# Causal self attention of layers 0 and 2: the mask before the row maximum added by VectorE instead of by identity products

## What is computed

```python
q, k, v = heads(x)                       # 8 batches, 16 heads, 256 rows, 8 columns; layer 2 rotates q and k
att = einsum('bhqd,bhkd->bhqk', q, k) * scale
att = where(causal, att, -inf)
att = softmax(att, axis=-1)              # the kernel takes the row maximum first and subtracts it
y = einsum('bhqk,bhkd->bhqd', att, v)
x = x + y @ w_out
```

## Time and profile before

| | us |
|---|---|
| median of 3 runs (1857.1 to 1859.6) | 1857.48 |
| the profiled execution, its own time | 1858.08 |
| its span in the profile | 1856.2 |
| TensorE busy in the span | 1498.0 |
| VectorE busy | 857.5 |
| ScalarE busy | 700.1 |
| GpSimd busy | 483.3 |

### The profile page before, as it was taken

How to read it: one execution, slowest core, us unless ns; L and a number is a source line. 1 busy time by engine, 2 the same in 40 slices (tenths; PEclk the granted TensorE clock), 3 DMA queues, 4 the chain that set the end, 5 groups by cost and what they waited for, 6 DMA issues and landing times. The chain is left out here.

```text
span 1856.2 us, 29632 instructions
## 1 busy us (share of the span) xinstructions
PE 1498.0 (81%) x10887; PEld 830.3 (45%) x10887; DVE 857.5 (46%) x2404; ACT 700.1 (38%) x1418; POOL 483.3 (26%) x566
## 2 busy tenths in 40 slices
PE   6899899995689999985998899973092579999876
PEld 4344344432544444454456344452071335555545
DVE  4555345542335555555312565355034645554244
ACT  2244414433137767562341143442031314343324
POOL 5533053310021111010001544100652435341034
PEclk9999999997999999986999999985595779999788
DMA  7800000000000000000002200000222000000012
GB/s 212 113 2 1 1 1 1 1 2 1 0 1 1 1 1 1 0 1 1 1 1 95 74 2 1 1 1 2 72 70 63 12 12 7 13 7 1 1 56 79
DMA packets 60258, 42.40 MB, mean 23 GB/s; under 512 B 13188, under 2 KB 54120, under 8 KB 60120
## 3 DMA queue, kind: packets, MB, share of 16 engines
q1 hardware_dynamic: 54752, 32.42, 7.1%
q0 software_dynamic: 3552, 7.33, 1.1%
q10 hardware_dynamic: 1816, 0.81, 0.2%
HBM read 25.88 MB, written 14.66 MB: 22 GB/s over the span
## 5 line engine op out<-in xcount | busy, mean ns | idle before, releaser
L1351 ACT ACTIVATE scores_L_experts_L<-L3x_psL 128x512 f32<-128x512 f32 x128 | 76.5, 597 | 173.2 <-PE L3x_psL L1214 169.5
L1388 DVE CUSTOM_DVE_ANT_0 L3x_junk<-L3x_psS,L3x_mask_rows 128x256 f32<-128x256 f32 x224 | 86.1, 421 | 92.4 <-PE L3x_psS L1176 84.0
L1214 PE MATMUL L3x_psL<-identb,L3x_mask_parts 128*128 128x256 bf16 x768 | 96.2, 276 | 0.0
L894 ACT ACTIVATE L0x_probs<-L0x_psL 128x512 f32<-128x512 f32 x96 | 52.1, 594 | 114.1 <-PE L0x_psL L707 78.9
L894 ACT ACTIVATE L2a_probs<-L2a_psL 128x512 f32<-128x512 f32 x96 | 52.1, 594 | 105.7 <-PE L2a_psL L705 70.9
L894 ACT ACTIVATE L0a_probs<-L0a_psL 128x512 f32<-128x512 f32 x96 | 52.1, 594 | 100.8 <-PE L0a_psL L705 65.0
L1196 PE MATMUL L3x_psL<-L3x_qm,ctx_T 32*128 32x512 f32 x256 | 73.3, 647 | 11.8 <-DVE L3x_mx L1388 11.3
L1214 PEld LDWEIGHTS L3x_psL<-identb,L3x_mask_parts 128*128 128x128 bf16 x768 | 70.4, 98 | 21.5 <-issue 13.7
L1625 PE MATMUL L1a_psL<-L1a_soft_near,neg_tri 128*128 128x512 f32 x128 | 67.9, 612 | 0.2 <-DVE L1a_soft_near L1832 0.2
L2907 POOL DMA_INDIRECT packed_rows<-h,slot x32 | 30.9, 964 | 141.7 <-POOLq L92 132.2
L1176 PE MATMUL L3x_psS<-L3x_km,L3x_qT 32*128 32x512 f32 x224 | 66.2, 668 | 1.9 <-DVE L3x_mx L1388 1.9
(11 more groups left out here) (800 smaller groups left out, 3917.6 us busy)
## 6 DMA issues: line engine op xcount, KB each, us to landing
L2f_rows<-packed_rows SPq DMA_DIRECT2D x8, 325.0 KB, 3.2
packed_rows<-zeros SPq DMA_DIRECT2D x1, 2560.0 KB, 28.2
experts_L_L<-in_L_ffn_w_dram SPq DMA_DIRECT2D x1, 2048.0 KB, 8.5
unpacked_rows<-zeros SPq DMA_DIRECT2D x1, 2048.0 KB, 18.0
scores_L_experts_L<-in_L_ffn_w_dram SPq DMA_DIRECT2D x1, 2048.0 KB, 7.9
L2f_back_rows<-unpacked_rows SPq DMA_DIRECT2D x16, 128.0 KB, 2.6
L3x_mask_rows<-in_mask_Bx1xSxS_ff_dram SPq DMA_DIRECT2D x8, 256.0 KB, 2.9
sorted_rows<-zeros SPq DMA_DIRECT2D x1, 1472.0 KB, 17.9
```

Of the source, the lines that this page charges most:

```text
L894: nc.scalar.activation(probs[:, half, a, k, :], psL[i % RING][:], ACT.Exp, scale=scale).then_inc(s_prob, 1)
L1214: last = nc.tensor.matmul(at[:, :, t * P:(t + 1) * P], parts[:, b % 2, i, t, u * P:(u + 1) * P], two, start=False, stop=i == PARTS - 1, sk ...
L1351: nc.scalar.activation(probs[:, half, a, k, :], psL[i % RING][:], ACT.Exp).then_inc(s_prob, 1)
L1388: last = nc.vector.tensor_tensor_reduce(out=junk[:, i, :], in0=psS[a][:, i * S:(i + 1) * S], in1=mrow[:, b % 2, t, :], scale=1.0, scalar=L ...
```

## The change

`quad_heads` gets an argument `hide_on_dve`, set for L0a and L2a and not for L0x. Where it is set, `hide_score` and the second half of `first_scores` issue nothing, and the products of q and k signal VectorE themselves. VectorE adds the mask to the bank while reading it and writes the sum to one buffer in SBUF, `hidden_scores` (128 x 512, float32); it waits for the add, and reduces the buffer. Before the next add it waits until that reduction is done, since there is one buffer. A new semaphore, `s_free`, counts the banks that have been read (by the add where there is one, by the reduction elsewhere), and TensorE waits for it in place of `s_red`.

```diff
 def quad_heads(nc, mem, w, name, *, ...
-               cross=False, mask, scale, loads=(), clear=()):
+               cross=False, mask, scale, hide_on_dve=False, loads=(), clear=()):
...
-        s_rq, s_rk = sem("q_roped"), sem("k_roped")
+        s_rq, s_rk, s_free = sem("q_roped"), sem("k_roped"), sem("score_bank_read")
+        hidden_scores = sb("hidden_scores", [P, 512]) if hide_on_dve else None
+        on_pe = [s is not None and not hide_on_dve for s in mask.scores]
+        on_dve = [s is not None and hide_on_dve for s in mask.scores]
...
                 def free_score_banks(m):
                     if m >= 1:
-                        pe.wait_ge(s_red, 2 * m)
+                        pe.wait_ge(s_free, 2 * m)
...
                 def hide_score(m, a):
-                    hidden = mask.scores[SCORE_AT[m % SLOTS][1]]
-                    if hidden is not None:
+                    k = SCORE_AT[m % SLOTS][1]
+                    hidden = mask.scores[k]
+                    if on_pe[k]:
                         nc.tensor.matmul(psS[a][:], mem.identb[:], hidden.unsqueeze(1).to_broadcast([P, 4, P]), start=False, stop=True,
                                          skip_group_check=True).then_inc(s_score, 1)
...
+                masked = [0]
+
+                def largest(dst, bank, k, m):
+                    heads = bank[:].rearrange("p (j n) -> p j n", j=4)
+                    if on_dve[k]:
+                        if masked[0]:
+                            dve.wait_ge(s_red, masked[0])
+                        masked[0] += 1
+                        at = hidden_scores[:].rearrange("p (j n) -> p j n", j=4)
+                        nc.vector.tensor_tensor(at, heads, mask.scores[k].unsqueeze(1).to_broadcast([P, 4, P]), ALU.add).then_inc(s_free, 1)
+                        dve.wait_ge(s_free, m + 1)
+                        nc.vector.tensor_reduce(dst, at, AX.X, ALU.max).then_inc(s_red, 1)
+                    else:
+                        nc.vector.tensor_reduce(dst, heads, AX.X, ALU.max).then_inc(s_free, 1)
...
-                        nc.vector.tensor_reduce(dst, psS[a][:].rearrange("p (j n) -> p j n", j=4), AX.X, ALU.max).then_inc(s_red, 1)
+                        largest(dst, psS[a], k, 2 * m + a)
...
                 def gather_max(b):
-                    dve.wait_ge(s_red, ITEMS * (b + 1))
+                    dve.wait_ge(s_free, ITEMS * (b + 1))
+                    if hide_on_dve:
+                        dve.wait_ge(s_red, 2 * sum(on_dve[k] for _, k in SCORE_AT) * (b + 1))
```

More of the change, by code:

```diff
@@ L645, in score @@
                     last = nc.tensor.matmul(psS[a][:], qT[rows, b % 3, t * P:(t + 1) * P], km[rows, b % 3, :, u * P:(u + 1) * P],
-                                            start=True, stop=mask.scores[k] is None, skip_group_check=True)
-                    if mask.scores[k] is None:
+                                            start=True, stop=not on_pe[k], skip_group_check=True)
+                    if not on_pe[k]:
                         last.then_inc(s_score, 1)
                 def hide_score(m, a):
-                    hidden = mask.scores[SCORE_AT[m % SLOTS][1]]
-                    if hidden is not None:
+                    k = SCORE_AT[m % SLOTS][1]
+                    hidden = mask.scores[k]
+                    if on_pe[k]:
                         nc.tensor.matmul(psS[a][:], mem.identb[:], hidden.unsqueeze(1).to_broadcast([P, 4, P]), start=False, stop=True,
@@ L659, in first_scores @@
                     else:
-                        pe.wait_ge(s_red, 4 * k)
+                        pe.wait_ge(s_free, 4 * k)
                     t, u = KINDS[k]
@@ L665, in first_scores @@
                         last = nc.tensor.matmul(first_banks[r][:], qT[rows, 0, t * P:(t + 1) * P], km[rows, 0, :, u * P:(u + 1) * P],
-                                                start=True, stop=hidden is None, skip_group_check=True)
-                        if hidden is None:
+                                                start=True, stop=not on_pe[k], skip_group_check=True)
+                        if not on_pe[k]:
                             last.then_inc(s_score, 1)
-                    if hidden is not None:
+                    if on_pe[k]:
                         for r in range(4):
@@ L3411, in decoder @@
         quad_heads(nc, mem, w, "L0a", wq=W0[:, 0:P], wk=W0[:, P:2 * P], wv=W0[:, 2 * P:3 * P], wo=w["L0_attn_w_proj"][:],
-                   bq=0, bk=1, bv=2, bo=0, mask=causal, scale=qk, loads=first_experts(w, dram),
+                   bq=0, bk=1, bv=2, bo=0, mask=causal, scale=qk, hide_on_dve=True, loads=first_experts(w, dram),
                    clear=blanks(w))
@@ L3431, in decoder @@
         quad_heads(nc, mem, w, "L2a", wq=w["L2_attn_Wq"][:], wq_rot=w["L2_attn_Wq_rot"][:], wk=w["L2_attn_Wk"][:],
-                   wk_rot=w["L2_attn_Wk_rot"][:], wv=w["L2_attn_Wv"][:], wo=w["L2_attn_Wo"][:], mask=causal, scale=qk, loads=last_experts(w, dram))
+                   wk_rot=w["L2_attn_Wk_rot"][:], wv=w["L2_attn_Wv"][:], wo=w["L2_attn_Wo"][:], mask=causal, scale=qk, hide_on_dve=True, loads=last_experts(w, dram))
         lone_head(nc, mem, w, "L2x", "causal")
```

2 lines of the change are left out of this document (1 added, 1 removed).

## The result

The changed kernel takes **1911.22 us** (median of 4 runs, 1909.8 to 1911.5) against 1857.81 beside it: a ratio of 1.0285, 95% interval 1.0267 to 1.0302. That is 53 us slower. The forecast was slower, by 24, and its range ended at 1896. The span of the profiled execution is 1908.4 us, 52.2 more than before.

What follows compares the result with a forecast made beforehand. The prediction took TensorE and VectorE to bound alternate slots in a chain. From 1858.1 us it added 21.2 for VectorE's longer chain and 4 for the clock, 1883.3, or 1882 by the median, range 1868 to 1896.

Steps and rivals of the forecast that it cites:

- Slots 2 and 4: Masked third and fifth of a batch's six slots: 3.46 us each, changes of -0.32 and -0.48 in a full batch.
- slot 5: A batch's last slot, where VectorE waits for TensorE to turn the maxima: 5.0 us instead of 4.30, +0.70.
- slot 0: A batch's first slot, delayed by the negation and the next add on VectorE: 4.65 us instead of 3.91, +0.74.
- I take 0.72 for a link that is waited for: VectorE's add-and-reduce chain: each operation whose result is waited for takes 0.72 us, the last 0.69.
- The walk: Slot-by-slot sum over a stage's seven batches: +6.2 us, with the stage's start +10.6 us a stage.
- the term of 21.2: VectorE's longer chain in L0a and L2a together, slots plus stage starts: +21.2 us.
- my 4.4: Start of each stage, groups of four banks up to the first slot: +4.4 us from later bank releases.
- 0.87 for an earlier start: First group of scores at a stage's start: VectorE begins 0.87 us earlier without the identity products.
- L2a has the same rows within 0.1: L2a assumed to match L0a's profile rows, so its +10.6 us was taken for both stages.
- I take the four long gaps alone at 1.0 each: TensorE's gaps of about 4.3 and 3.25 us at each stage's start drop its clock: +4 us in all.
- the clock falls at most turns as well: Rival: TensorE's clock also falls at most turns of the maxima, 21.2 + 25 us, 1904; chance 0.11.
- GpSimd rival: GpSimd's writes slow VectorE's new SBUF traffic, 0.1 us more per link, +47 us, 1906; chance 0.03.

Runs made afterwards that it cites:

- e6: Changed kernel plus dummy TensorE products at the start of L0a and L2a and before slot 0 of every batch, the last included: 1886.82 us, ratio 1.0140.
- e2: Changed kernel with VectorE waiting for both banks of a masked pair at once and for the turn only once: 1899.22 us, a single run.
- e1: Changed kernel plus dummy TensorE products at the start of L0a and L2a and before slot 0 of each batch except the last: 1901.81 us, ratio 1.0236.
- e9: Kernel before the change, plus one waited bank copy on VectorE between the turn of the maxima and slot 5's reductions in L0a and L2a: 1884.28 us, ratio 1.0126.
- e8: Kernel before the change, mask still on TensorE, with two alternating sets of maxima so slot 5's reductions need not wait for the turn: 1842.97 us, ratio 0.9900.
- e11: Changed kernel with adds before the turn, negation ahead of reductions, later h in slot 1, dummies at stage start, and L0x's mask on VectorE too: 1814.25 us, ratio 0.9760.
- e3: Changed kernel with two bf16 buffers, so VectorE does both adds of a pair and then both reductions, all after the turn's wait: 1870.09 us, ratio 1.0068.
- e5: As e3, but the wait for the turn of the maxima moved behind the adds, in front of the reductions: 1847.05 us, ratio 0.9943.

## Why the prediction was wrong, step by step

**Right: the sign and the mechanism of the chain.** TensorE and VectorE bound alternate slots, and the bank's release became add, reduction, add. Slots 2 and 4 were put at 3.46 and measured 3.54 and 3.49; slot 5 at 5.0 and measured 5.14; the wait at the turn at 2.2 and measured 2.26; slot 0, without the clock, at 4.65 and measured 4.65 in batch 1 and 4.86 in batches 2 to 4 (e6). The page of the Trainium skill, "VectorE: DVE Perf Modes" (the section on the DRAIN), by which a semaphore behind each operation costs nothing, would have made the links 0.60. They are 0.72 and more, as rows 4 against rows 3 said.

**Wrong, the smaller part: "I take 0.72 for a link that is waited for".** Rows 4 show a link with one wait ahead of it. Half of the new links have two or three, 0.79 and 0.82 by the timeline, 0.72 again in e2. The walk with these values gives about 13 a stage, where I had 10.6; e1 measured 13.2 in L0a and e6 12.5 in L2a. So the term of 21.2 should have been 25.7. It was sized from the right row but for the wrong number of waits, which the code of `largest` and `reduce` shows. The links are not all of it: in L0a the start of the stage took 5.5 for my 4.4, most of that since "0.87 for an earlier start" came out as 0.26. That L2a has the same rows within 0.1 was wrong as well, but without weight: its slot 1 took 3.25 where L0a's took 2.63, before and after.

**Wrong, the larger part: "I take the four long gaps alone at 1.0 each", +4 in the sum.** Measured: 22.0. The step that failed is to put the falls at the turns at nothing. Behind all 14 turns some of slots 0 and 1 ran at the lower clock. Against e6, slots 0 and 1 cost 7.1 us more in L0a and 7.8 in L2a, about 1.06 a turn; the other 7 lie mostly ahead of the first slot, which comes 2.1 and 3.3 us earlier after the first warm-up product in e6.

The rival "the clock falls at most turns as well", at 0.11, was the true case. Its 21.2 + 25 comes near the 25.7 + 22.0 measured in the two stages only since its chain was too small and its price of a fall, 1.54, too high. (The 1906 of the GpSimd rival lies nearer still to 1911, by luck: the operations kept their 0.69, and e2 gave the links back their 0.72.) The price of 1.54 holds where TensorE bounds the slot (e9); where VectorE's chain bounds it, part of a slow stretch is hidden, down to 0.03 in one batch of L2a. I argued "the price is too high where the slot waits for VectorE anyway" and took from this that the falls would hardly count. Half the argument was sound; the conclusion wasn't.

The list of gaps also left out the first turn of each stage, 2.48 long in the changed kernel, with a slot 0 of 4.68 behind it (4.07 in e6). The trace before had the warning: one fall in 14 turns at gaps of 1.3 to 1.5, with the gaps about to grow by 0.9. And a second one that I overlooked, behind the last turn of L0x:

```profile
399.30 0.70 PE L679 MATMUL L0x_psL<-L0x_qm,L0x_kT 32*128 32x512 f32 x2 [1.54 <-DVE L0x_mx L954]
...
404.04 0.70 PE L679 MATMUL L0x_psL<-L0x_qm,L0x_kT 32*128 32x512 f32 x2
...
400.00:402.00 2.00, 2.00 (x12) 0.26 (x6) 0.84 (x2) 0.00 (x0) 0.00 (x0) 0.50 0.00 0
```

With it, of six turns with a gap of 1.54 or 1.55 two drew a fall, and of fifteen with 1.32 none. I treated a draw that had come out badly as rare when its odds were about to change.

The page "TensorE: Matmul & The Clock Gate", Part 1, in the Trainium skill, makes the slow clock the idle state. Used for the four long gaps alone it agreed with my term. The trace agrees that the falls at the turns stand behind idle time, and shows them behind gaps well under the long ones at the start (5.06 and 3.48): 2.05 us drew one in eight of ten cases (e9).

**Open.** The 4.5 us outside the two stages aren't explained; unchanged code varies by that much, so I give them no cause. Why the clock of L2a's last batch fell in e1, and stayed down, isn't explained either.

## What to carry to other kernels

Before work goes to an engine with a low busy share, find whose *release* it will stand in: here a release that came 0.92 us later outweighed a saving of 0.54 a pair, and with the same added operations in another order (adds, then what others wait for, then reductions) the loss became a gain of 25 us. Ask of such a gain how much of it the change itself has: 16 of the 25 came with the mask left on TensorE (e8). Count the wait instructions ahead of a link in the code, and price a link by a row that has as many. And if a wait of TensorE grows where a trace shows even one fall of its clock, price the falls at every such wait and put that case in the forecast, not among the rivals.

## What the runs showed of the hardware

- A second wait instruction on VectorE costs 0.07 us in a chain that is bound by dependencies (0.72 to 0.79), a third 0.03 more (0.82), though what the later ones wait for had long come. Merged waits give it back (e2).
- An operation of 128x512 on VectorE takes 0.69 from a bank or from SBUF, and two in a row of bf16 from SBUF take 1.27 against 1.29 for float32 from banks: neither the place nor the type mattered here.
- TensorE's clock behind a turn, in L0a and L2a: before, ten gaps of 1.32 drew no fall and four of 1.54 one. In e9 ten of 2.05 drew eight and four of 2.27 three. In e2 and in the changed kernel all 28, of 2.16 to 2.48, drew some 1.2 GHz. L0x, whose code only e11 changed, says the same over the other 11 traces: 55 gaps of 1.32 drew none and 22 of 1.54 or 1.55 nine, at 1.4 to 1.6 us each. A gap of 1.31 with a second of 1.07 behind it drew falls in six of the ten full batches (e3), 0.59 to 0.63 with the same 1.07 in none (e5).
- In e1 the clock stayed at 0.50 from about 1220 us through L2a's last batch and on to about 1271. Over 20 us of that (1222 to 1242) TensorE was busy 4.00 of every 4.00 us. No other run did that behind a turn. A busy engine was not enough to come back soon there; what else it takes, these runs don't tell.
